# Two value tiles of cross-attention issued between the first attends instead of ahead of them

## The chip, the cores and the metric

The kernel runs on one core of a Trainium2 chip. The metric is the device time of one execution in microseconds (us). The engines named below are TensorE (PE in the rows, with its weight loads listed apart as PEld), VectorE (DVE), ScalarE (ACT), GpSimd (POOL), and SyncE (SP), which issues the DMAs. Every engine runs its own instructions in the order in which the program lists them, and the engines are held together by semaphores.

## The reference, cut to what matters

A decoder block of three parts, each followed by a layer normalisation, on `x` of 8 x 128 tokens with 512 channels: causal self-attention with 4-bit weights, cross-attention with 16 heads, and a gated expert layer. The change lies in the second part:

```python
def proj(x, W, bias):
    y = x @ W.T + bias
    return y.reshape(b, s, head_num, hd).transpose(0, 2, 1, 3).reshape(b * head_num, s, hd)
Q = proj(q, Wq, bq)
K = proj(k, Wk, bk)
V = proj(v, Wv, bv)
scores = jnp.einsum('bqd,bkd->bqk', Q, K) / jnp.sqrt(jnp.asarray(hd, jnp.float32))
attn = jax.nn.softmax(scores, axis=0)
res = jnp.einsum('bqk,bkd->bqd', attn, V)
out = res.reshape(b, head_num, s, hd).transpose(0, 2, 3, 1).reshape(b, s, hd * head_num)
```

Here `b` = 8, `s` = 128, `hd` = 32. The softmax is taken over the 128 pairs of batch entry and head (axis 0), so no tile of probabilities can be weighted before the exponentials of all eight tiles have been summed. Afterwards `x = _layernorm(x + out)`, and the third part follows:

```python
x = _layernorm(x + _L0_ffn_ref(x, ...), axis=-1)
```

## The kernel before, in words

The tokens are cut into NB = 8 tiles of 128 tokens, one for each batch entry. Self-attention takes the first three quarters of the span. In cross-attention the keys and queries are projected, the scores of the eight tiles are made (`scores2`), and VectorE takes the maxima, the shifts and the sums of the exponentials. Its chain ends in the reciprocal (L1382) and one product (L1383). Each engine's order is written out by hand; there is no planner around the change.

The parts that the steps of the prediction touch:

- **values(b)** (L1743, its matmuls at L1753) on TensorE makes the value tile b: 128 tokens by 512 channels, four fp32 matmuls, which the trace lists as eight records of 128x512. Tiles 0 to 2 take their bias from a matmul with ones (L1749). Tiles 3 to 7 add to a PSUM bank that ScalarE has filled with the bias (`seed_bias`, L1000). The bank is `proj2_bank(16 + b)`, one of banks 0 to 2 in turn. Before the change all eight are issued in a row after the last scores.
- **copy_v2(b)** (L1006, its instruction at L1010) on ScalarE copies the bank into `v2` and raises `proj2_copied`.
- **weigh(b)** (L1385, L1386) on VectorE multiplies the 128x2048 exponentials of tile b by the reciprocal sums and raises `weights2_ready`.
- **attend(b)** (L1847, L1855) on TensorE waits for `weights2_ready`, for `proj2_copied`, and for the copy of attended tile b - 2. It makes the attended tile in bank 6 or bank 4, as 32 records of 128x128.
- **copy_att(b)** (L1092, L1095) on ScalarE copies the attended tile to SBUF.
- **turn_att(b)** (L1859, L1864) on TensorE waits for that copy and for the adding of attended tile b - 1, and transposes the tile into bank 7, as four records.
- **add_attended(b)** (L1389, L1392) on VectorE waits for the transposes (`att_turned`) and adds the tile to `y`.
- **layernorm_stats** (L1274, L1278), **inverse_deviation** on GpSimd (L749, L752) and **layernorm_apply** (L1286) normalise two tiles at a time.
- **turn_x(1, b)** (L1713) transposes the normalised tile, `copy_x_t` (L981) copies it, and **gate_and_lora** (L1871) and **main** (L1880) are the first products of the expert layer.
- On SyncE the loads of the expert layer's weights (L603 to L605) wait until all 24 projection units, the eight value tiles being the last of them, are done (`proj2_done`, L602). TensorE waits for these three loads before `gate_and_lora(0)`.

VectorE's order in this stretch fixes what a late attended tile delays:

```python
weigh(0)
weigh(1)
for b in range(2, NB):
    weigh(b)
    add_attended(b - 2)
    if b % 2 == 1:
        layernorm_stats(1, b - 3, 2, attended2)
    elif b > 2:
        layernorm_apply(1, b - 4, 2)
```

So `add_attended(0)` stands behind `weigh(2)` and ahead of `weigh(3)`, and `add_attended(1)` stands behind `weigh(3)`, ahead of the first statistics and of `weigh(4)`.

Of the kernel before, what the change touches and what calls it, by code (L numbers as in the profile page):

```python
# [17 lines left out]
NB = 8  # L18
# [44 lines left out]
def wait(eng, sem, value):  # L63

    if isinstance(value, int) and value <= 0:
        return
    eng.wait_ge(sem, value)


def build(nc, t, out):  # L70
    with ExitStack() as ctx:
# [383 lines left out]
        def att_bank(b):  # L455

            return banks[6 if b % 2 == 0 else 4]
# [15 lines left out]
        def proj2_bank(i):  # L473

            if i < KC:
                return banks[7]
            if i < 2 * KC:
                return banks[(3, 4, 0, 1)[i - KC]]
            return banks[i % 3]
# [290 lines left out]
        def _(act):  # L770
# [225 lines left out]
            def exps2(b):  # L996
                act.wait_ge(shifted2, b + 1)
                nc.scalar.activation(xs[:, SLOT[b], :], xs[:, SLOT[b], :], ACT.Exp, scale=XSCALE).then_inc(exp2_done, 1)

            def seed_bias(b):  # L1000

                i = 4 * KC + b
                wait(act, proj2_copied, i - 2)
                nc.scalar.activation(proj2_bank(i), bias_v, ACT.Copy).then_inc(bias_seeded, 1)

            def copy_v2(b):  # L1006

                i = 4 * KC + b
                act.wait_ge(proj2_done, UNIT_ORDER.index(i) + 1)
                nc.scalar.activation(v2[:, b, :], proj2_bank(i), ACT.Copy).then_inc(proj2_copied, 1)  # L1010
# [73 lines left out]
            copy_v2(2)  # L1084
            seed_bias(5)
            exps2(7)
            for b in range(3, NB):
                copy_v2(b)
                if b + 3 < NB:
                    seed_bias(b + 3)  # L1090

            def copy_att(b):  # L1092
                act.wait_ge(pv2_done, b + 1)
                wait(act, att_turned, b - 1)
                nc.scalar.activation(att_t[:, b % 2, :], att_bank(b), ACT.Copy).then_inc(att_copied, 1)  # L1095

            for b in range(5):
                copy_att(b)
            copy_x_t(1, 0, x3_t)
            copy_x_t(1, 1, x3_t)  # L1100
# [415 lines left out]
        def _(pe):  # L1516
# [226 lines left out]
            def values(b):  # L1743

                i = 4 * KC + b
                first = b < 3
                if first:
                    wait(pe, proj2_copied, i - 2)
                    nc.tensor.matmul(proj2_bank(i), ones[0:1, :], bias_v[0:1, :], start=True, stop=False)  # L1749
                else:  # L1750
                    wait(pe, bias_seeded, b - 2)
                for g in range(KC):
                    mm = nc.tensor.matmul(proj2_bank(i), ctx_t[:, g, b * P:(b + 1) * P], wv2[:, g, :],  # L1753
                                          start=False, stop=not first or g == KC - 1, skip_group_check=not first)
                mm.then_inc(proj2_done, 1)
# [85 lines left out]
            for b in range(BPH):  # L1841
                scores2(BPH + b)
            pe.wait_ge(scores2_copied, NB - 1)
            for b in range(NB):
                values(b)

            def attend(b):  # L1847

                pe.wait_ge(weights2_ready, b + 1)
                pe.wait_ge(proj2_copied, 4 * KC + b + 1)  # L1850
                wait(pe, att_copied, b - 1)
                for n in range(KC):
                    for i in range(4):
                        h = 4 * n + i
                        mm = nc.tensor.matmul(att_bank(b)[32 * i:32 * i + 32, n * P:(n + 1) * P], v2[:, b, h * XD:(h + 1) * XD],  # L1855
                                              xs[:, SLOT[b], (KC * i + n) * P:(KC * i + n + 1) * P], start=True, stop=True)
                mm.then_inc(pv2_done, 1)

            def turn_att(b):  # L1859

                pe.wait_ge(att_copied, b + 1)
                wait(pe, attended2, b)
                for n in range(KC):
                    mm = nc.tensor.transpose(banks[7][:, n * P:(n + 1) * P], att_t[:, b % 2, n * P:(n + 1) * P], ident)  # L1864
                mm.then_inc(att_turned, 1)
# [23 lines left out]
                                 start=False, stop=True).then_inc(main_done, 1)  # L1889

            attend(0)
            attend(1)
            turn_att(0)
            attend(2)
            turn_att(1)
            attend(3)
# [134 lines left out]
```

## Time and profile before

| what | value |
|---|---|
| median of 3 runs | 679.2 us (676.06 to 680.47) |
| profiled execution, its own time | 676.55 us |
| its span in the trace | 674.8 us |
| TensorE busy | 639.5 us (95%) |
| VectorE busy | 556.5 us (82%) |
| ScalarE busy | 465.8 us (69%) |
| GpSimd busy | 420.9 us (62%) |
| mean granted TensorE clock | 0.992 of full speed |

All times inside the kernel are us from the start of the span. The span leaves out 1.75 us of the execution's own time. Busy shares are means over a span whose parts have different limits, so the stretch around the change is read by itself, in the rows further down.

### The profile page before, as it was taken

The numbers are of one execution on the slowest core, as the hardware profiler recorded it, in microseconds if no ns is written. First come the engines' busy times: TensorE is split into PE (matmuls) and PEld (weight loads), VectorE is DVE, ScalarE is ACT, GpSimd is POOL, SyncE is SP. The second block draws the span as 40 slices with busy tenths as digits, with TensorE's granted clock in tenths as the row PEclk, the third lists the DMA queues.
The fourth block names the chain that finished last, engine by engine and source line by source line (L and its number), as shares of the span: only waits on it lengthen the run. The fifth ranks groups of instructions, "written<-read, shape, count | busy, mean of one in ns | idle before, by whom it ended". The sixth has DMA issues, their size and how long they took to land.

```text
span 674.8 us, 11004 instructions
## 1 busy us (share of the span) xinstructions
PE 639.5 (95%) x3294; PEld 444.9 (66%) x3294; DVE 556.5 (82%) x880; ACT 465.8 (69%) x1271; POOL 420.9 (62%) x372
## 2 busy tenths in 40 slices
PE   8989999999999999999999999998998999978996
PEld 4566787877878777787777877765565444447552
DVE  5878999998999999999899989974462968998357
ACT  6697887979779797797977979776644545622100
POOL 2478899899899989989989998881230000012003
PEclk9999999999999999999999999999999998999998
DMA  7864523533351351253234124240010000020003
GB/s 232 261 166 114 154 69 96 151 109 94 110 141 46 88 165 33 59 153 90 60 111 132 43 61 114 89 127 0 1 63 0 1 1 1 0 98 2 0 1 124
DMA packets 30187, 56.72 MB, mean 84 GB/s; under 512 B 4784, under 2 KB 5040, under 8 KB 29616
## 3 DMA queue, kind: packets, MB, share of 16 engines
q1 hardware_dynamic: 30128, 56.02, 29.4%
q8 instruction: 27, 0.44, 0.3%
q14 instruction: 32, 0.26, 0.1%
HBM read 32.93 MB, written 2.10 MB: 52 GB/s over the span
## 4 chain that ended last, share of the span: by engine, by line
PE 76%; DVE 9%; ACT 4%; issue 3%; POOL 3%; DMA 2%; SPq 1%; POOLq 0%; DVEq 0%; ACTq 0%
PE ps L1527 23%; PE ps L1589 18%; PE ps L1570 8%; PE ps L1542 8%; PE ps L1597 6%; PE ps L1552 4%; PE ps L1880 3%; DMA arena<-in_qkv 2%; DVE arena L1386 2%; ACT arena L993 1%; PE ps L1770 1%; DVE arena L1359 1%; DVE late L1354 1%; DVE late L1367 1%; PE ps L1871 1%
## 5 line engine op out<-in xcount | busy, mean ns | idle before, releaser
L1140 DVE SCALAR_TENSOR_TENSOR arena<-ps,arena 128x512 f32<-128x512 f32 x288 | 212.5, 745 | 15.7 <-PE ps L1527 3.8
L1527 PE MATMUL ps<-x_hi,w_sb 128*128 128x512 f32 x384 | 170.9, 445 | 5.1 <-ACT arena L790 2.2
L1527 PE MATMUL ps<-x_lo,w_sb 128*128 128x512 f32 x384 | 150.8, 393 | 0.0
L1168 DVE SCALAR_TENSOR_TENSOR y<-ps,arena,y 128x512 f32<-128x512 f32 x192 | 138.2, 744 | 12.6 <-PE ps L1589 8.5
L799 ACT ACTIVATE arena<-ps,small 128x128 f32<-128x128 f32 x256 | 90.7, 378 | 31.3 <-DVE small L1146 26.8
L624 POOL TENSOR_TENSOR arena<-arena,consts 128x512 f32<-128x512 f32 x75 | 96.9, 1291 | 22.7 <-DVE arena L1140 22.7
L1589 PE MATMUL ps<-heads_hi,wo_sb 128*128 128x512 f32 x256 | 108.7, 425 | 0.1
L630 POOL TENSOR_TENSOR arena<-arena,consts 128x512 f32<-128x512 f32 x75 | 96.8, 1290 | 12.6 <-DMA arena<-arena 10.4
L749 POOL TENSOR_SCALAR var_eps<-mean_var 128x2 f32<-128x2 f32 (+1 forms) x13 | 7.3, 561 | 154.4 <-DVE mean_var L1278 154.4
L1589 PE MATMUL ps<-heads_lo,wo_sb 128*128 128x512 f32 x256 | 101.0, 395 | 0.0
L640 POOL TENSOR_TENSOR arena<-arena 128x512 f32<-128x512 f32 x75 | 96.6, 1287 | 5.6
L648 POOL TENSOR_TENSOR y<-arena,y 128x512 f32<-128x512 f32 x64 | 82.6, 1290 | 26.6 <-ACT arena L840 24.5
L1527 PEld LDWEIGHTS ps<-x_hi,w_sb 128*128 128x128 f32 x384 | 72.2, 188 | 39.0 <-DVE arena L1140 8.7
L790 ACT ACTIVATE arena<-ps,arena 128x512 f32<-128x512 f32 x96 | 66.6, 694 | 34.1 <-PE ps L1527 33.5
L1527 PEld LDWEIGHTS ps<-x_lo,w_sb 128*128 128x128 f32 x384 | 72.5, 189 | 16.5 <-issue 5.5
L816 ACT ACTIVATE arena<-arena,small 128x128 f32<-128x128 f32 x256 | 82.6, 419 | 0.2 <-DVE small L1152 0.2
L1570 PE MATMUL ps<-arena 128*128 128x512 f32 x128 | 66.2, 599 | 4.3 <-ACT arena L823 2.2
L1542 PEld LDWEIGHTS ps<-arena 128*128 128x128 f32 x512 | 66.2, 193 | 5.7 <-issue 1.9
L1542 PE MATMUL ps<-arena 128*128 128x128 f32 x512 | 68.0, 276 | 0.5 <-POOL arena L640 0.5
L1159 DVE TENSOR_TENSOR heads_lo<-ps,heads_hi 128x512 fp32r<-128x512 f32 x64 | 44.1, 689 | 24.4 <-ACT heads_hi L832 23.9
L1589 PEld LDWEIGHTS ps<-heads_hi,wo_sb 128*128 128x128 f32 x256 | 48.5, 189 | 16.7 <-DVE heads_lo L1159 5.6
L799 ACT ACTIVATION_READ_ACCUMULATOR arena<-ps,small 128x1 f32 x256 | 55.8, 218 | 0.0
(146 smaller groups left out, 967.6 us busy)
## 6 DMA issues: line engine op xcount, KB each, us to landing
arena<-arena SPq DMA_DIRECT2D x160, 128.0 KB, 2.3
arena<-in_qkv SPq DMA_DIRECT2D x48, 256.0 KB, 3.9
arena<-in_o SPq DMA_DIRECT2D x32, 256.0 KB, 3.7
arena<-in_x_t SPq DMA_DIRECT2D x8, 256.0 KB, 3.7
y<-in_x SPq DMA_DIRECT2D x4, 512.0 KB, 4.4
arena<-in_ctx_t SPq DMA_DIRECT2D x8, 256.0 KB, 3.1
out<-y SPq DMA_DIRECT2D x8, 256.0 KB, 2.1
arena<-in_wk SPq DMA_DIRECT2D x1, 1024.0 KB, 5.2
```

Source lines behind the costliest of these rows:

```text
L624: nc.gpsimd.tensor_tensor(by_tile(raw_cos[:, i % 2, :]), by_tile(raw[:, c % RING, :]), every_tile(cos_of(c)), ALU.mult).then_inc(cos_done, 1)
L630: nc.gpsimd.tensor_tensor(by_tile(turned[:, i % 2, :]), by_tile(turned[:, i % 2, :]), every_tile(sin_of(c)), ALU.mult).then_inc(sin_done, 1)
L640: nc.gpsimd.tensor_tensor(dst, raw_cos[:, i % 2, :], turned[:, i % 2, :], ALU.add).then_inc(rotated, 1)
L648: nc.gpsimd.tensor_tensor(dst, by_tile(out_part[:, k % 2, :]), dst, ALU.add).then_inc(part_added, 1)
L799: last = nc.scalar.activation(probs[:, s, h, :], score_ps[s][:, h * P:(h + 1) * P], ACT.Exp, bias=neg_max[:, s, h:h + 1], accum_out=row_su ...
L816: last = nc.scalar.activation(probs[:, s, h, :], probs[:, s, h, :], ACT.Copy, scale=row_inv[:, s, h:h + 1])
L1140: nc.vector.scalar_tensor_tensor(acc, group_bank(p, KC * c + g), scale_of(p // 2, c, g), acc, ALU.mult, ALU.add).then_inc(dve_scaled, 1)
L1168: nc.vector.scalar_tensor_tensor(dst, by_tile(out_bank(p, u)), out_scale_of(p // 2, u), dst, ALU.mult, ALU.add).then_inc(out_added, 1)
L1527: mm = nc.tensor.matmul(group_bank(p, u), w_sb[:, c, g, :], part[:, g, half * HALF:(half + 1) * HALF], start=(k == 0), stop=(k == 1))
L1542: mm = nc.tensor.matmul(score_ps[s][:, h * P:(h + 1) * P], q_t[:, h, b * P:(b + 1) * P], k_t[:, b * P:(b + 1) * P], start=False, stop=(n > ...
L1570: nc.tensor.matmul(pv_ps[:, :], v_sb[:, b, :], probs_t[:, s, :, :].rearrange("p h q -> p (h q)"), start=True, stop=True).then_inc(pv_done, 1)
L1589: mm = nc.tensor.matmul(out_bank(p, u), wo_sb[:, h, nt * P:(nt + 1) * P], part[:, half, h, :], start=(k == 0), stop=(k == 1))
```

## The change

On TensorE, `values(6)` moves from ahead of `attend(0)` to behind it, and `values(7)` from ahead of `attend(0)` to behind `turn_att(0)`. On ScalarE, `copy_v2(6)` moves behind `copy_att(0)` and `copy_v2(7)` behind `copy_att(1)`. `seed_bias(6)` and `seed_bias(7)` stay where they were. No instruction is added or removed, and VectorE's, GpSimd's and SyncE's programs are unchanged.

```diff
@@ ScalarE
-            for b in range(3, NB):
+            for b in range(3, 6):
                 copy_v2(b)
                 if b + 3 < NB:
                     seed_bias(b + 3)
@@
-            for b in range(5):
+            copy_att(0)
+            copy_v2(6)
+            copy_att(1)
+            copy_v2(7)
+            for b in range(2, 5):
                 copy_att(b)
@@ TensorE
-            for b in range(NB):
+            for b in range(6):
                 values(b)
@@
             attend(0)
+            values(6)
             attend(1)
             turn_att(0)
+            values(7)
             attend(2)
             turn_att(1)
             attend(3)
```

## Rows read from the trace of the kernel before

**Rows 1.** The page: busy us, share of the span, instructions; then the ending chain's shares.

```profile
PE 639.5 (95%) x3294; PEld 444.9 (66%) x3294; DVE 556.5 (82%) x880; ACT 465.8 (69%) x1271; POOL 420.9 (62%) x372
...
PE 76%; DVE 9%; ACT 4%; issue 3%; POOL 3%; DMA 2%; SPq 1%; POOLq 0%; DVEq 0%; ACTq 0%
```

**Rows 2.** The chain that ended last, 586 to 616: start, duration, what.

```profile
589.71 6.69 DVE arena L1386 x3
596.41 0.60 DVE y L1392
597.01 2.20 DVE arena L1386
599.21 0.60 DVE y L1392
...
601.30 2.15 POOL var_eps L749
...
609.56 2.15 POOL var_eps L749
...
612.51 0.56 DVE y L1286
...
613.11 0.67 PE ps L1713 x4
```

**Rows 3.** Timeline of TensorE, 572 to 606: start, duration, instruction, idle before.

```profile
572.71 20.87 PE L1753 MATMUL ps<-arena 128*128 128x512 f32 x48
593.51 1.95 PE L1855 MATMUL ps<-arena 128*32 128x128 f32 x64
595.39 0.66 PE L1864 MATMUL ps<-consts,late 128*128 128x128 f32 x4
596.46 1.08 PE L1855 MATMUL ps<-arena 128*32 128x128 f32 x32 [0.41 <-DVE arena L1386]
597.47 0.66 PE L1864 MATMUL ps<-consts,late 128*128 128x128 f32 x4
599.26 1.08 PE L1855 MATMUL ps<-arena 128*32 128x128 f32 x32 [1.13 <-DVE arena L1386]
...
603.45 1.08 PE L1855 MATMUL ps<-arena 128*32 128x128 f32 x32 [2.52 <-DVE arena L1386]
```

**Rows 4.** Busy time by stretch: length, engines, granted clock, DMA share, GB/s.

```profile
469.50:472.90 3.40, 3.40 (x15) 3.01 (x13) 0.75 (x1) 0.83 (x2) 0.06 (x1) 0.50 0.00 0
561.65:565.07 3.42, 3.42 (x5) 1.51 (x5) 3.39 (x2) 0.69 (x1) 0.00 (x0) 0.50 0.00 0
...
599.20:602.60 3.40, 1.67 (x36) 1.24 (x36) 3.40 (x7) 0.60 (x1) 1.30 (x1) 1.00 0.04 13
...
668.70:670.90 2.20, 0.00 (x0) 0.00 (x0) 1.99 (x5) 0.00 (x0) 0.83 (x2) 1.00 0.64 238
670.90:674.80 3.90, 0.00 (x0) 0.00 (x0) 0.65 (x2) 0.00 (x0) 0.70 (x2) 0.50 0.36 134
```

**Rows 5.** Timeline of TensorE: a gap in self-attention, then value tiles 0 and 1.

```profile
468.42 1.12 PE L1570 MATMUL ps<-arena 128*128 128x512 f32 x2 [2.15 <-ACT arena L823]
...
561.68 5.37 PE L1753 MATMUL ps<-arena 128*128 128x512 f32 x8
...
568.03 3.70 PE L1753 MATMUL ps<-arena 128*128 128x512 f32 x8
```

**Rows 6.** The expert weights' last load and its landing, and the first gate product.

```profile
L605 SPq DMA_DIRECT2D arena<-in_w_b x1: 432/432/432, 594.5 to 594.5; - x1
...
DMA to landing us min/median/max: 5.4/5.4/5.4
...
606.76 1.25 PE L1871 MATMUL ps<-arena 128*128 128x160 f32 x8
```

**Rows 7.** Busy time by stretch, columns as in rows 4: the attends, the expert layer.

```profile
593.50:613.10 19.60, 13.55 (x269) 10.88 (x268) 19.07 (x23) 5.63 (x10) 5.67 (x4) 1.00 0.23 85
613.10:654.70 41.60, 38.97 (x213) 25.39 (x213) 22.46 (x75) 6.49 (x13) 3.41 (x5) 1.00 0.00 1
```

## The prediction

> **What bounds the kernel now.** I read the page first. TensorE is busy for 95% of the span and carries 76% of the chain that ended last [rows 1], which would suggest that anything that frees TensorE pays. But that is a mean over the whole span, and the change sits in one stretch of 20 us, so the second view is the chain in order of time around it. There the end is not set by TensorE: from 589.71 to 613.07 the chain lies on VectorE, with two visits to GpSimd for the deviations (the one at 601.30 and a second like it at 609.56), and TensorE takes it over only at 613.11 [rows 2]. What the reader is to see in that view is the order weigh(0), weigh(1), weigh(2) (6.69 us for the three), add_attended(0), weigh(3), add_attended(1), with no gap between them. The third view, the sums by stretch, says the same: from 593.5 to 613.1 VectorE is busy for 19.07 of 19.60 us and TensorE for 13.55; from 613.1 to 654.7 it is TensorE with 38.97 of 41.60 [rows 7]. The fourth view is TensorE's own timeline, for how near it runs to the chain. Value tiles 2 to 7 end at 593.51, where attend(0) starts at once, and turn_att(0) runs from 595.39 to 596.05 [rows 3]. VectorE is free for add_attended(0) at 596.41. So the transposed tile 0 is ready only 0.36 us before it is wanted, and tile 1 (597.47 to 598.13) 1.08 us before 599.21 [rows 2, 3]. Whatever is put ahead of these two transposes on TensorE beyond that slack is paid by VectorE.
>
> **What the change takes away.** Six value tiles, 48 records, take 593.51 - 572.71 = 20.80 us, or 3.47 us each [rows 3]. With tiles 6 and 7 moved, the values end at 593.51 - 6.93 = 586.58. Can this pull anything forward? attend(0) needs weigh(0), which starts at 589.71 and takes 6.69 / 3 = 2.23 us, so it ends at 591.94 and attend(0) can start at about 592.00, 1.5 us earlier than before. Nothing on the chain follows from that, since add_attended(0) stands behind weigh(2), which ends at 596.40 whatever TensorE does. VectorE's softmax chain does not read the value tiles, so weigh(0) doesn't come earlier. The part that is removed is worth 0, and it opens a gap on TensorE from 586.58 to 592.00, 5.4 us.
>
> **What it adds, at full clock.** The pair of attends takes 1.95 us for 64 records, so one holds TensorE for 0.98 us [rows 3]. attend(0) runs from 592.00 and values(6) from 592.98 to 596.45, which passes the end of weigh(2). Then attend(1) holds TensorE to 597.43, and turn_att(0), which now stands behind both, takes 0.66 us and ends at 598.09. add_attended(0) starts then instead of at 596.41: VectorE stands still for 1.7 us. Next, the issue of turn_att(0) frees TensorE after 0.6 us, at 598.0; values(7) runs to 601.5, attend(2) to 602.5, and turn_att(1) ends at 603.1. On VectorE add_attended(0) and weigh(3) take 0.60 + 2.20 us [rows 2] and end at 600.9, so add_attended(1) waits another 2.2 us, and starts at 603.15 instead of 599.21. The delay is now 3.9 us. It isn't 2 x 3.47, because the 1.5 us by which attend(0) starts earlier and the slack of 1.1 us before add_attended(1) come off, and some of the seams differ by tenths; I take **+4.0**.
>
> Behind add_attended(1) nothing makes it good. VectorE goes on with the statistics of tiles 0 and 1, weigh(4) and the rest in the same order, each of which was back to back before [rows 2, 7]; GpSimd starts from those statistics; attend(4) waits for weigh(4), as before (its idle of 2.52 us was ended by VectorE) [rows 3]; and turn_x(1, 2) at 613.11, from which TensorE sets the end, is released by the normalising at 612.51 [rows 2]. From there to the end TensorE is almost full, so the delay goes through one to one.
>
> **ScalarE and SyncE.** Each copy_v2 now stands in front of one copy_att. copy_v2(6) waits for values(6), and attend(1) is behind values(6) on TensorE anyway, so copy_att(1) isn't later for it; the same holds for copy_v2(7) and copy_att(2). Cost 0, covered by TensorE's own order. If that cover failed, 0.6 us a copy would be the price. The loads of the expert weights are issued when the last value tile is done: that moves from 593.5 to 601.5, by 8 us. Before, the last of the three was issued at 594.5 and landed 5.4 us later, at 599.9, and the gate product that needs it began at 606.76 [rows 6]. After, it lands at 607.9 at full clock and the gate product is due at 606.76 + 4.0 = 610.8. The slack shrinks from 6.9 to 2.9 us but is not gone. Cost 0; with a landing twice as long, 5.4 us more, it would be 2.5.
>
> **The clock.** The 5.4 us gap is new, and it has a price of its own. In self-attention a gap of 2.15 us before 468.42 was followed by the lower level (0.50, 1.2 GHz) from 469.50 to 472.90, and after the last matmul the clock was at 0.50 from 670.90, 2.2 us into the idle time. Against that, the idle of 2.52 us before 603.45 cost nothing: the clock stayed at 1.00 (2.4 GHz) [rows 3, 4, 5]. So gaps of this size go either way; one of 5.4 us, twice as long as any of the three, I expect to bring the clock down. Its price comes from value tile 0, which ran in such a stretch: 5.37 us against 3.70 us for tile 1 at full clock, **+1.67 us** [rows 4, 5]. Both low stretches with dense work in them lasted 3.4 us. If the whole of such a stretch falls on attend(0) and values(6), all of 1.67 us goes in front of turn_att(0) and so into the chain. Bounds: 0 from below (no fall, as before 603.45), and twice 1.67 = 3.3 from above (still low after the first stretch, as at the end of the trace, where it is at 0.50 for 3.90 us with no matmul). I take 1.67, the row with dense work.
>
> How this weighs for attend(0), no row shows, as no attend ran at the lower clock. The Trainium skill, page "TensorE: Matmul & The Clock Gate", section "Wait — 56ns, not 53.3ns?", gives a floor of about 25 ns from one start to the next for small matmuls; attend's records come every 0.98 us / 32 = 31 ns, near it. By that rule attend(0) would not slow down, and of the 3.4 us low only the 2.4 us in values(6) would cost, half of them: an estimate of 1.2 us in place of 1.67. The sum would be 0.5 us smaller; the sum below doesn't use it.
>
> **Sum.** 0 (removed) + 4.0 (two transposes late) + 1.7 (clock) = +5.7 us. Against the profiled execution's own time, 676.55 + 5.7 = 682.3. That execution is on the low side of the runs shown (676.06, 679.2, 680.47). With it there are four, whose middle is (676.55 + 679.2) / 2 = 677.9; +5.7 gives **683.5 us**, 0.8% more. A change of 1%, 6.8 us, is about what a measurement of this kernel can tell from none.
>
> **The rivals.**
>
> A, *the clock stays up*: only the +4.0. For it: the 2.52 us gap without a fall. Against it: the new gap is over twice that. Time 677.9 + 4.0 = 681.9. Chance 0.13.
>
> B, *a second fall of the clock*. The gap before attend(4), 2.5 us long, stays, and now comes after other work, so that it may be judged as the 2.15 us gap was. Or the first low stretch runs longer. Another 1.67 on attend(4) and what follows, or in the dense part after 613: 677.9 + 4.0 + 3.3 = 685.2, slower by 1.1%. For it: the gaps of 1.13 and 2.52 us in this part [rows 3]. Against it: neither brought a fall before. Chance 0.18.
>
> C, *the other side: TensorE's idle time swallows the two tiles*. TensorE has 19.60 - 13.55 = 6.05 us idle between 593.5 and 613.1 [rows 7], nearly the 6.93 us of two tiles, and attend(0) starts 1.5 us earlier. The place is the wait of add_attended(0), and the point from which it decides is 596.41: if turn_att(0) were through by then and turn_att(1) by 599.21, VectorE would lose nothing, and if the early attends then let TensorE run ahead, up to 1.5 us would be won, 677.9 - 1.5 = 676.4. Against it: turn_att(0) stands behind values(6) in program order, values(6) alone ends at 596.45, and the idle time lies mostly after 600. Chance 0.06, gain and no change together.
>
> D, *the expert weights come late*: the gate product waits for the loads. Its point is a landing after 610.8; the slack is 2.9 us, and the delay on both sides grows alike with the clock. With a landing twice as long +2.5 us: 686.0. Chance 0.03.
>
> **How the numbers follow.** My forecast has 0.60, A 0.13, B 0.18, C 0.06, D 0.03. The forecast at +5.7, with the clock's price anywhere from 0.8 to 2.5, lies just below the 6.8 us of 1%, so about a quarter of it (0.14) comes out slower by over 1%; with 0.13 of B's 0.18 and D's 0.03 that makes 0.30. Faster by over 1% would need more than any step can give: 0.02. The rest, 0.68, is within 1%. The range goes from A less the spread of the runs (681.9 - 2.9 = 679.0) to the far end of the clock with that spread, 677.9 + 4.0 + 3.3 + 2.3 = 687.5. It leaves out most of C.
>
> **What would show it right or wrong.** In the profile after: attend(0) starts near 592.0 with an idle time of about 5 us before it, released by VectorE's weigh(0); the granted clock is at 0.50 for a stretch around 590 to 596; add_attended(0) and add_attended(1) show idle times before them, released by TensorE's L1864, of about 1.7 and 2.2 us at full clock, together 3.5 to 5.7 with the clock's part; turn_x(1, 2) comes 4 to 7.5 us after 613.11; what lies behind it keeps its length. The prediction is wrong if VectorE shows no such waits, if the gate product waits for a DMA, or if the part behind turn_x(1, 2) gets shorter by what was lost.

## The result, and the profile after

The changed kernel takes 685.45 us (median of 4 runs, 684.27 to 685.6) against 678.36 us for the kernel before (median of 4, 676.06 to 680.47): 7.1 us more. The ratio is 1.0102, with a 95% interval of 1.0077 to 1.0127. The profiled execution took 685.44 us, its span is 683.7 us. The forecast was 683.5 us in a range of 679.0 to 687.5.

The page of the kernel after, busy time by engine and the shares of the ending chain, beside [rows 1]:

```profile
PE 643.3 (94%) x3294; PEld 447.3 (65%) x3294; DVE 557.2 (82%) x880; ACT 466.1 (68%) x1271; POOL 421.4 (62%) x372
...
PE 77%; DVE 8%; ACT 4%; issue 3%; POOL 3%; DMA 2%; SPq 1%; POOLq 0%; DVEq 0%; ACTq 0%
```

The same instructions run; TensorE is busy 3.8 us longer for the same work, which already hints at a lower clock. The chain that ended last shows where the time is (line numbers behind the edit are 4 higher than before):

```profile
591.50 2.30 DVE arena L1390
593.80 0.04 issue
593.84 1.94 PE ps L1859 x32
595.78 5.53 PE ps L1757 x8
601.31 1.01 PE ps L1859 x32
602.32 0.59 PE ps L1868 x4
602.91 3.44 PE ps L1757 x8
606.34 1.01 PE ps L1859 x32
607.35 0.60 PE ps L1868 x4
607.95 0.02 issue
607.98 0.69 DVE y L1396
...
621.98 0.67 PE ps L1717 x4
```

Before, this stretch was VectorE alone: three weighs, add_attended(0), weigh(3), add_attended(1) [rows 2]. Now it goes from weigh(0) through attend(0), values(6), attend(1), turn_att(0), values(7), attend(2) and turn_att(1), all on TensorE, and returns to VectorE at add_attended(1). A chain that moves to another engine for 14 us is the sign of a wait that was not there before. The timeline of VectorE shows the two waits by name; the bracket is the idle time and what ended it:

```profile
591.50 6.70 DVE L1390 TENSOR_TENSOR arena<-arena,small 128x2048 f32<-128x2048 f32 x3
602.94 0.69 DVE L1396 TENSOR_TENSOR y<-ps,y 128x512 f32<-128x512 f32 x1 [4.75 <-PE ps L1868]
603.55 2.28 DVE L1390 TENSOR_TENSOR arena<-arena,small 128x2048 f32<-128x2048 f32 x1
607.98 0.69 DVE L1396 TENSOR_TENSOR y<-ps,y 128x512 f32<-128x512 f32 x1 [2.14 <-PE ps L1868]
```

4.75 + 2.14 = 6.9 us of VectorE's time, ended by the transposes of turn_att(0) and turn_att(1). TensorE's timeline shows the gap that the moved tiles left, 7.01 us, and values(6) behind it:

```profile
572.83 14.00 PE L1757 MATMUL ps<-arena 128*128 128x512 f32 x32
593.84 1.94 PE L1859 MATMUL ps<-arena 128*32 128x128 f32 x32 [7.01 <-DVE arena L1390]
595.71 5.60 PE L1757 MATMUL ps<-arena 128*128 128x512 f32 x8
601.24 1.08 PE L1859 MATMUL ps<-arena 128*32 128x128 f32 x32
602.25 0.66 PE L1868 MATMUL ps<-consts,late 128*128 128x128 f32 x4
602.74 3.60 PE L1757 MATMUL ps<-arena 128*128 128x512 f32 x8
```

attend(0) takes 1.94 us where attend(1) takes 1.08, and values(6) 5.60 us where values(7) takes 3.60. The sums by stretch say why; columns as in [rows 4], the granted clock third from the end:

```profile
586.80:589.30 2.50, 0.03 (x1) 0.00 (x0) 2.40 (x4) 0.60 (x1) 0.00 (x0) 1.00 0.00 0
589.30:593.80 4.50, 0.00 (x0) 0.00 (x0) 4.33 (x7) 0.00 (x0) 0.00 (x0) 0.50 0.00 0
593.80:599.50 5.70, 5.66 (x37) 3.12 (x38) 4.39 (x2) 0.60 (x1) 0.00 (x0) 0.50 0.00 0
599.60:608.00 8.40, 8.40 (x88) 4.40 (x91) 2.92 (x3) 2.37 (x4) 0.00 (x0) 1.00 0.06 12
613.30:616.60 3.30, 3.00 (x17) 2.59 (x14) 3.30 (x4) 1.20 (x2) 0.00 (x0) 0.50 0.00 2
```

The clock fell to 0.50 (1.2 GHz) some 2.5 us into the gap, and stayed there for the first 5.7 us of the work behind it.

**A measure that scatters less than the span.** I cut each span in three: up to the start of weigh(0), from there to the start of turn_x(1, 2), where TensorE takes over for good, and the rest. Before, that is 589.71, 23.40 and 61.7 us; after, 591.50, 30.48 and 61.7 us. The middle part grew by 7.08 us. The span grew by 8.9 us because this execution also came to weigh(0) 1.79 us later; whether that belongs to the change is one of the things tested below.

### The profile page after: what moved, and what is told of

It is laid out like the page before. It is cut to its first block, busy times and chain, and to the rows that moved or that the text cites. A ratio compares the mean times of both kernels' runs of the same rounds, so it can differ in the third digit from the quotient of the medians.

```text
span 683.7 us, 11004 instructions
## 1 busy us (share of the span) xinstructions
PE 643.3 (94%) x3294; PEld 447.3 (65%) x3294; DVE 557.2 (82%) x880; ACT 466.1 (68%) x1271; POOL 421.4 (62%) x372
## 4 chain that ended last, share of the span: by engine, by line
PE 77%; DVE 8%; ACT 4%; issue 3%; POOL 3%; DMA 2%; SPq 1%; POOLq 0%; DVEq 0%; ACTq 0%
PE ps L1531 23%; PE ps L1593 17%; PE ps L1574 8%; PE ps L1546 8%; PE ps L1601 6%; PE ps L1556 4%; PE ps L1884 3%; DMA arena<-in_qkv 2%; ACT arena L993 1%; PE ps L1757 1%; DVE arena L1363 1%; PE ps L1774 1%; DVE late L1358 1%; DVE late L1371 1%; PE ps L1875 1%
## 5 line engine op out<-in xcount | busy, mean ns | idle before, releaser
L630 POOL TENSOR_TENSOR arena<-arena,consts 128x512 f32<-128x512 f32 x75 | 96.9, 1292 | 14.5 <-DMA arena<-arena 13.1
```

What stands on the lines that cost most here:

```text
L630: nc.gpsimd.tensor_tensor(by_tile(turned[:, i % 2, :]), by_tile(turned[:, i % 2, :]), every_tile(sin_of(c)), ALU.mult).then_inc(sin_done, 1)
```

## The experiments

Theory: two costs, nothing else. The order costs about 4 us, because turn_att(0) and turn_att(1) now stand behind value tiles and VectorE waits for them; the clock costs about 3 us, because the gap brings it down. Rivals: the order alone costs 7 us and the clock nothing; TensorE is the bound here and any work moved costs its length; a part of the 7 us arises ahead of weigh(0). All kernels ran beside the kernel before. "Stretch" is weigh(0) to turn_x(1, 2); each row is one profiled execution, all columns in us.

| kernel | weigh(0) starts | to add_attended(0) | on to add_attended(1) | stretch | rest |
|---|---|---|---|---|---|
| before | 589.71 | 6.62 | 2.80 | 23.40 | 61.7 |
| before, again | 592.61 | 6.62 | 2.79 | 23.41 | 61.7 |
| after | 591.50 | 11.44 | 5.04 | 30.48 | 61.7 |
| after, again | 592.15 | 11.68 | 5.04 | 30.71 | 61.6 |
| after, gap filled | 593.40 | 8.70 | 5.03 | 27.73 | 61.7 |
| tile 7 alone, behind turn_att(0) | 593.18 | 6.61 | 4.68 | 25.29 | 61.6 |
| tile 7 alone, behind turn_att(1) | 590.75 | 7.57 | 2.80 | 24.36 | 61.7 |
| tile 6 alone | 591.45 | 11.59 | 2.81 | 28.39 | 61.7 |
| tile 6 alone, gap filled | 593.88 | 8.70 | 2.80 | 25.49 | 61.6 |
| tiles 6 and 7 left out | 591.82 | 7.17 | 2.80 | 23.96 | 61.6 |
| GpSimd weighs tiles 3 and 5 | 593.65 | 15.26 | 3.15 | 32.94 | 61.3 |
| the same, tile 7 behind turn_att(1) | 592.36 | 15.26 | 3.15 | 34.96 | 61.4 |

**1. The gap filled.** The kernel after, with matmuls that keep TensorE at work:

```diff
+            for k in range(6):
+                nc.tensor.matmul(banks[3], ctx_t[:, k % KC, 0:P], wv2[:, k % KC, :], start=True, stop=True)
             attend(0)
             values(6)
```

> The kernel after, with six fp32 matmuls of 128x512 into the free bank 3 (0.86 us each, 5.1 us) between value tile 5 and attend(0), where TensorE stood idle for 7.0 us. Their results are not used. Theory (two causes, order and clock): the granted clock stays at 1.00 up to attend(0) and behind it, attend(0) takes 1.0 us and values(6) 3.4 us instead of 1.94 and 5.53; the stretch from the start of weigh(0) to the start of turn_x(1, 2), 23.40 us before and 30.48 us after, is 27.5 us; the time is 4.1 us over the kernel before. Rival (order alone; the low clock costs nothing on the path): 30.5 us and +7.1 us.

Measured: 684.26 us against 679.0, ratio 1.0071 (1.0051 to 1.0091). The stretch is 27.73 us, 2.75 us shorter than after and 4.33 us longer than before. TensorE's timeline in this kernel, from the filler on:

```profile
588.57 5.31 PE L1896 MATMUL ps<-arena 128*128 128x512 f32 x12
595.75 1.08 PE L1859 MATMUL ps<-arena 128*32 128x128 f32 x32 [1.87 <-DVE arena L1390]
596.76 3.70 PE L1757 MATMUL ps<-arena 128*128 128x512 f32 x8
```

and its sums by stretch, with the clock at 1.00 in both:

```profile
593.90:595.70 1.80, 0.00 (x0) 0.00 (x0) 1.80 (x2) 0.00 (x0) 0.00 (x0) 1.00 0.00 0
595.70:602.10 6.40, 6.35 (x77) 3.75 (x78) 4.40 (x2) 1.75 (x3) 0.00 (x0) 1.00 0.00 0
```

attend(0) is back at 1.08 us and values(6) at 3.70 us, with more work on TensorE than before. This run separates the two costs: the order 4.3 us, the clock 2.75 us. A kernel that does more is faster by 2.75 us in the stretch. On the medians the two kernels lie about 2 us apart (+7.1 and +5.3), with intervals that overlap, so the size of each cost rests on the stretches. The interval by itself, +3.5 to +6.2 us, holds the 4.1 us of the theory and not the 7.1 us of the rival.

**2. Tile 7 alone, behind turn_att(0).**

```diff
-            for b in range(NB):
+            for b in range(7):
                 values(b)
@@
             attend(1)
             turn_att(0)
+            values(7)
             attend(2)
```

> Only value tile 7 is moved, behind turn_att(0) as in the change; tile 6 is made ahead of attend(0) as before. Theory: turn_att(0) is on time, turn_att(1) is about 1.75 us late for add_attended(1); the gap before attend(0) is 3.5 us or less, so a fall of the clock adds between 0 and 1.7 us: +1.7 to +3.4 us, the stretch from weigh(0) to turn_x(1, 2) 25.1 to 26.8 us. Rival (all of the change's cost comes from values(6) ahead of attend(1)): +0.

Measured: 681.89 us against 679.0, ratio 1.005 (1.0033 to 1.0068); stretch +1.89 us. In the profiled execution the gap before attend(0) was only 1.89 us, since value tile 0 had run at the lower clock (5.40 us in place of 3.70) and ended the value tiles later; behind the gap the clock stayed up. add_attended(0) is on time, add_attended(1) is 1.88 us late. So values(6) is not the whole cost. The interval, +2.2 to +4.6 us, lies above this one stretch.

**3. Tile 7 alone, behind turn_att(1).** The edit is the same but for the place (copy_v2(7) moves with it, behind copy_att(2)):

```diff
             turn_att(0)
             attend(2)
             turn_att(1)
+            values(7)
             attend(3)
```

> Only value tile 7 is moved, but behind turn_att(1) instead of turn_att(0); the gap ahead of attend(0) is the same as in the run with tile 7 behind turn_att(0). Theory (what counts is what stands ahead of a transpose that VectorE waits for): turn_att(1) has 1.1 us of slack, turn_att(2) ends 0.1 us before it is wanted, so 0 at full clock and up to +1.2 with a low stretch of the clock. Rival (a tile moved out of the front costs its 3.5 us wherever it stands, as TensorE is the bound): +1.7 to +3.5 us.

Measured: 678.12 us against 679.0, ratio 0.9992 (0.998 to 1.0003): no difference. The same tile leaves the same place and costs nothing in the runs, one transpose further down: what counts is what stands ahead of a transpose that VectorE waits for. The gap was not the same as in the last run, as its text had assumed: here value tile 0 ran at full clock, and the gap was 3.58 us. It was followed by a low clock, which made turn_att(0) late by 0.87 us; that is the +0.96 us of this stretch. TensorE's timeline holds one more thing:

```profile
593.09 1.93 PE L1858 MATMUL ps<-arena 128*32 128x128 f32 x32 [3.58 <-DVE arena L1389]
...
609.92 1.35 PE L1874 MATMUL ps<-arena 128*128 128x160 f32 x8 [1.00 <-DMA arena<-in_w_b]
```

The first gate product (L1874) waits 1.00 us for the last of the expert weights, whose load was issued at 604.5 and not at 594.5. That is the wait of my rival D. It costs nothing here: VectorE shows no wait for TensorE in this part, and the rest behind turn_x(1, 2) keeps its 61.7 us.

**4. Tiles 6 and 7 left out.** The kernel before without the eight fp32 matmuls of value tiles 6 and 7; their banks are copied with the bias alone. The two waits for all 24 units, on SyncE and on ScalarE, are lowered to 22, and only the first is shown. The kernel leaves out a part of the result.

```diff
-            for b in range(NB):
+            for b in range(6):
                 values(b)
@@
-            sp.wait_ge(proj2_done, UNITS)
+            sp.wait_ge(proj2_done, UNITS - 2)
```

> The kernel before, with value tiles 6 and 7 not computed at all (their banks, holding the bias alone, are copied), so that attend(0) follows value tile 5: 6.9 us less work on TensorE and the same gap before attend(0) as in the kernel after. Theory (VectorE is the bound from weigh(0) to turn_x(1, 2)): no gain, -0.5 to +1.0 us, where a cost comes from attend(0) and attend(1) at the lower clock. Rival (TensorE, 95% busy, is the bound here too): -6.9 us.

Measured: 678.91 us against 679.0, ratio 0.9995 (0.9978 to 1.0012). 6.9 us of TensorE's work less buys nothing (the interval is -1.5 to +0.8 us): VectorE is the bound in this stretch, and TensorE's 95% on the page says nothing about it. The stretch is +0.56 us, from a low clock behind a gap of 5.32 us, which made turn_att(0) late by 0.47 us:

```profile
594.17 1.93 PE L1857 MATMUL ps<-arena 128*32 128x128 f32 x32 [5.32 <-DVE arena L1388]
596.37 1.93 PE L1857 MATMUL ps<-arena 128*32 128x128 f32 x32 [0.27 <-DVE arena L1388]
```

**5. Tile 6 alone, between attend(0) and attend(1).** Tile 7 is made ahead of attend(0); the order of the units and of the copies follows.

```diff
-UNIT_ORDER = list(range(UNITS))
+UNIT_ORDER = list(range(UNITS - 2)) + [23, 22]
@@
-            for b in range(NB):
+            for b in [0, 1, 2, 3, 4, 5, 7]:
                 values(b)
@@
             attend(0)
+            values(6)
             attend(1)
```

> Only value tile 6 is moved, between attend(0) and attend(1); tile 7 is made ahead of attend(0), in front of it. Theory: turn_att(0) is 1.7 us late for add_attended(0); the 1.1 us of slack before add_attended(1) and the rest of the order hide nothing of it, since VectorE runs back to back behind it; the gap before attend(0) is 1.9 to 3.5 us, so up to 1.7 us more for the clock: +1.7 to +3.4 us, the stretch from weigh(0) to turn_x(1, 2) 25.1 to 26.8 us. Together with the +1.9 us of tile 7 alone that gives less than the 4.3 us of both at full clock. Rival (one tile is swallowed by the gap it leaves, 1.5 us earlier start of attend(0)): +0.

Measured: 682.86 us against 678.39, ratio 1.0066 (1.0045 to 1.0087); stretch +4.99 us. That is above what the theory allowed. The clock was low behind a gap of 3.58 us, and attend(0) and values(6) took 1.93 and 5.75 us, so most of the surplus looked like the clock; I had allowed 1.7 us for it. The next run tests that.

**6. Tile 6 alone with the gap filled.** The same with three such filler matmuls ahead of attend(0).

> Value tile 6 alone moved between attend(0) and attend(1), with three fp32 matmuls of 128x512 into the free bank 3 (2.6 us) in the gap before attend(0); their results are not used. Theory: the gap shrinks from 3.6 to about 1 us, the clock stays at 1.00, attend(0) takes 1.0 us and values(6) 3.4 us in place of 1.93 and 5.75: the stretch from weigh(0) to turn_x(1, 2) is 25.2 us in place of 28.39, the time +1.8 us over before. Rival (the order alone makes the 5.0 us of this tile): 28.4 us and +4.5 us.

Measured: 681.45 us against 678.38, ratio 1.0042 (1.0025 to 1.0059); stretch 25.49 us, +2.09. The clock stayed up behind a gap of 1.01 us, and attend(0) and values(6) took 1.08 and 3.70 us. So for tile 6 the order costs 2.1 us and the clock 28.39 - 25.49 = 2.9 us. The medians lie closer together, +4.5 and +3.1 us; the second interval, +1.7 to +4.0 us, leaves out the 4.5 us of the rival. At full clock tile 6 costs 2.1, tile 7 1.9, and both together 4.3 us.

**7. The kernels before and after once more.**

> The kernel before, unchanged, for a second profile of it. Theory (the start of weigh(0) scatters from run to run, whatever the order behind it, and the first profile of before was an early one): weigh(0) starts between 591 and 593.5 us, later than 589.71, and the stretch from there to turn_x(1, 2) is 23.4 us again, with 61.7 us behind it. Rival (the change also delays what stands ahead of weigh(0)): weigh(0) starts near 589.7 again.

> The kernel after, unchanged, on the same chip as the three others. Theory: +7 us as in the first measurement, the stretch from weigh(0) to turn_x(1, 2) about 30.5 us with a low clock behind the gap; the clock's part can differ from run to run between 1.2 and 3.1 us, so 28.8 to 30.7. Rival (the first measurement's 3 us for the clock was chance): under 29 us and +5 us.

Measured: before, 679.47 us, one run; weigh(0) starts at 592.61, the stretch is 23.41 us. After, 686.56 us against 678.39, ratio 1.0105 (1.008 to 1.0131); weigh(0) at 592.15, stretch 30.71 us, attend(0) at 1.94 and values(6) at 5.83 us. The kernel before came to weigh(0) later in its second profile, at 592.61, than the kernel after in either of its own. So the 1.79 us ahead of weigh(0) is no cost of the change, and the first profile of before was the earliest of all (the table has 589.71 to 593.88). That is why I had to set its time beside the median. The stretch and the rest repeat within 0.3 us in the two profiles that each of these kernels has.

What the stretches leave open is 1 to 2 us in the time of a whole execution. The second comparison of after gives +8.2 us on the medians and +7.1 by its ratio, and its six runs split into four of 686.3 to 687.8 us and two of 682.9 and 683.2. With the gap filled the medians are 1 us above the stretch, for both tiles (+5.3 and +4.33) and for tile 6 (+3.1 and +2.09). For tile 7 alone the whole interval misses the stretch, above it behind turn_att(0) (+2.2 to +4.6, stretch +1.89) and below it behind turn_att(1) (-1.4 to +0.2, stretch +0.96). Other executions may have had another clock, or another start of weigh(0); no run here separates the two.

**8. VectorE relieved.** Since VectorE is the bound, I gave two of its eight weighs to GpSimd, which stands idle there, on top of the kernel before (attend(3) and attend(5) then wait for GpSimd, which is not shown):

```diff
+            pool.wait_ge(soft_step, 33)
+            for b in (3, 5):
+                weighed = xs[:, SLOT[b], :].rearrange("p (g q) -> p g q", q=P)
+                nc.gpsimd.tensor_tensor(weighed, weighed, x_r[b // BPH].unsqueeze(1).broadcast_to([P, 16, P]),
+                                        ALU.mult).then_inc(pool_weighed, 1)
@@
-                weigh(b)
+                if b not in (3, 5):
+                    weigh(b)
```

> The kernel before, with weigh(3) and weigh(5) taken from VectorE and done by GpSimd, which stood idle up to 601: both 128x2048, of four 128x512 at 1.29 us each, so some 5.2 us a tile, done 10.3 us after the sums are ready. Theory (VectorE sets the pace from weigh(0) to turn_x(1, 2)): add_attended(1) comes about 1 us earlier, held then by turn_att(1), and weigh(5) leaves 2.2 us less behind it: the stretch falls from 23.4 to 20.3 us, -2 to -3.2 us. Rival (TensorE sets it): 0. Second rival (the two engines slow each other on SBUF): weigh on VectorE takes clearly longer than 2.2 us and the gain goes.

> Both together: weigh(3) and weigh(5) on GpSimd, and value tile 7 behind turn_att(1). Theory: once VectorE is relieved, turn_att(2) behind value tile 7 is what is late, so the tile costs 0 to 1 us at full clock and up to 1.7 us more with the clock low; -0.5 to -3 us against the kernel before, no better than the run with GpSimd alone. Rival (a relieved VectorE makes TensorE the bound and the late tile pays for its 1.5 us earlier start): better than GpSimd alone by 1 us or more.

Measured: 689.19 us against 678.39, ratio 1.0142 (1.0123 to 1.0161), and with the late tile 7 690.35 us, ratio 1.0168 (1.0153 to 1.0184). The gain that both texts expected did not come; the second rival of the first text holds. The late tile made nothing better, so the rival of the second text falls. Its stretch is 2.0 us longer, and here the chain that ended last runs through the late loads: values(7), then the last load of expert weights with 5.47 us to its landing, then the first gate product, which waited 1.49 us for it. The timeline of GpSimd and VectorE in the first of the two:

```profile
593.65 15.34 DVE L1392 TENSOR_TENSOR arena<-arena,small 128x2048 f32<-128x2048 f32 x3
593.69 13.15 POOL L765 TENSOR_TENSOR arena<-arena,small 128x2048 f32<-128x2048 f32 x2 [79.86 <-DVE small L1389]
```

The same three weighs on VectorE take 6.70 us in the kernel after and 15.34 us here. This says nothing against VectorE being the bound. The three weighs became 8.64 us longer, the two that left VectorE took some 4.4 us off, and two waits for transposes behind attends at the lower clock, of 2.47 and 2.05 us, came on: 8.8 of the 9.5 us by which the stretch grew. It only shows that GpSimd cannot take this work from VectorE in this form. No version was faster than the kernel before by more than the noise.

## Why the prediction was right, point by point

- **VectorE bounds the stretch, TensorE only from turn_x(1, 2).** Right. 6.9 us of TensorE's work left out gained nothing, and the rest behind turn_x(1, 2) is 61.6 to 61.7 us in every order of the attends, so the delay goes through one to one.
- **What is removed is worth 0.** Right, by the same run.
- **The waits.** They came where the prediction put them, ended by the transposes. Their sum, 4.75 + 2.14 = 6.9 us, is above the 3.5 to 5.7 that it gave as a sign, and the surplus is the clock's, below.
- **The order, +4.0.** It measured 4.3 us at full clock. The waits of VectorE are 2.00 us for add_attended(0), where I had 1.7, and 2.14 for add_attended(1), where I had 2.2; the rest is in the seams. One reason that I gave is a chance of one profile: attend(0) could start 1.5 us earlier only because the value tiles had ended late in it. In the second profile of before, attend(0) already started 2.35 us behind the start of weigh(0), as it does after the change (2.34). The slack ahead of the two transposes was the same there, 0.4 and 1.0 us, and it is the slack that sets the cost.
- **The clock, +1.67.** The fall came as forecast, but its size was too small: 2.75 us in the first profile, by the run with the gap filled, and about 2.9 us for tile 6 alone. Two things went wrong in "I take 1.67, the row with dense work". The gap is 7.0 us and not 5.4: in the first profile of before, value tile 0 ran at the lower clock, which put the end of all value tiles 1.67 us late; in the kernel after it did not. And I took over the length of a low stretch, 3.4 us, with all of it on dense work. Here it lasted from 589.3 to about 599.6, of which the last 5.7 us fell on work; half of that is 2.85 us. In the second profile of after, the fall came some 3 us into the gap, 6.1 us of work were at the lower clock, and attend(0) and values(6) took 0.2 us more. The price lies inside my bounds of 0 and 3.3.
- **attend(0) at the lower clock.** The Trainium skill, page "TensorE: Matmul & The Clock Gate", section "Wait — 56ns, not 53.3ns?", gives the floor of about 25 ns between starts; that attends at 31 ns a record would therefore keep their pace at the lower clock was my reading of it. attend(0) went from 1.08 to 1.94 us, so the row decides against that reading, and the sum was right not to use it.
- **The sum.** 4.3 + 2.75 = 7.05 us, measured 7.09 on the medians; that they agree to the tenth is luck, as the medians of the second comparison differ by 8.2. My +5.7 was 1.4 short: 1.1 of it the clock, 0.3 the order. The rest of the distance to 685.45 is my starting point, 677.9, where the kernel before measured 678.36. The longer low stretch is rival B in its second form, "the first low stretch runs longer", whose 685.2 us is nearer to the 685.45 measured than the 683.5 of the likeliest case.
- **Rival B, a second fall.** It came too, from 613.3 to 616.6, and cost nothing: VectorE shows no wait for TensorE there. I had priced it as if every low stretch were on the chain.
- **The chances.** I gave 0.68 to a change within 1% and 0.30 to one slower by more. The ratio is 1.0102 (1.0077 to 1.0127), on the edge and by its middle on the less likely side. That 1% is about what a measurement of this kernel can tell from none was too cautious: with 4 to 12 runs the intervals here reach 0.12 to 0.26% to either side.
- **Rival A**, the clock stays up, is what the filler makes: 27.73 us. **Rival C** fell, since the transposes were not through in time. **Rival D** did not occur in the kernel after: the loads landed at 607.2 + 6.8 = 614.0 us and the gate product came at 616.50. The wait did show with tile 7 behind turn_att(1): off the chain on the kernel before, and on the chain together with GpSimd's weighs.
- **ScalarE, cost 0.** Right: copy_v2(6) and copy_v2(7) end before the attended tile they stand ahead of is there.

## What to carry to other kernels

Before work is moved "into idle time" of a busy engine, look for the transposes or copies behind the place that another, fully loaded engine waits for, and compare their slack (here 0.36 and 1.08 us) with the length of what is put ahead of them; one place further down the same tile cost nothing. Price the hole it leaves as well: here each of the six gaps of 3.58 us or more before attend(0) brought TensorE's clock down, and the work behind it paid. And where the whole span scatters by 4 us, measure the change in the stretch between two fixed instructions, which repeated here within 0.3 us, and keep the medians beside it: a stretch is one execution, with the clock that this one happened to have.

## What the runs showed of the hardware that I had not expected

**The clock behind gaps.** In the profiles, gaps on TensorE of 1.01, 1.87 and 1.89 us before attend(0) left it at 1.00. Gaps of 3.58 (three times), 5.32 and 7.01 us (twice) each brought it to 0.50. The low stretches lasted 10.2 us behind the longest gaps and 6.8 us behind the shorter ones, but for one gap of 3.58 us that was soon followed by a second of 4.58 us, again 10.2 us. Gaps of 2.5 to 2.8 us before attend(4) went both ways, for the same program: no fall in the first profile of before, a fall in the second. A long gap isn't even needed. In 3 of the 12 profiles (before, tile 7 alone behind turn_att(0), tiles 6 and 7 left out) the clock was at 0.50 for the 3.4 us of value tile 0, behind idle times of 1.1 us at most between the last scores; in the other 9, with the same instructions up to there, it was not. This decides whether the value tiles ahead of attend(0) end 1.7 us later, and with it how long the gap before attend(0) is. Work of all shapes slowed: attend from 1.08 to 1.94 us, values(6) from 3.70 to 5.60 us with some two thirds of it at the lower clock.

**VectorE and GpSimd on SBUF.** A weigh reads two operands from SBUF. With GpSimd doing the same beside it, the two engines took turns. The starts of the attends show when each weigh of VectorE ended in that run:

```profile
596.00 1.08 PE L1864 MATMUL ps<-arena 128*32 128x128 f32 x32
...
602.52 1.94 PE L1864 MATMUL ps<-arena 128*32 128x128 f32 x32 [5.44 <-DVE arena L1392]
...
609.04 1.93 PE L1864 MATMUL ps<-arena 128*32 128x128 f32 x32 [3.56 <-DVE arena L1392]
```

weigh(0) ended just before 596.00, after its usual 2.3 us, although GpSimd had begun 0.04 us behind it; weigh(1) and weigh(2) came 6.5 us apart each. The two tiles of GpSimd took 13.15 / 2 = 6.6 us each. If a weigh of VectorE needs 2.23 us alone, 6.5 - 2.23 = 4.3 us are left for one of GpSimd. This 4.3 is an estimate, as no run has GpSimd weighing alone. By strict turns each tile of GpSimd then waits for one weigh of VectorE, 2 x (2.23 + 4.3) = 13.1 us, where 13.15 were measured. Sharing by halves would have slowed weigh(0) too. The second run with GpSimd repeats both totals, 15.34 and 13.15 us. The Trainium skill, page "SBUF — State Buffer", section "SBUF: two separate sides", states that a VectorE instruction with two SBUF inputs, against a GpSimd instruction that reads SBUF, takes a shared pair of ports exclusively, and that whichever starts first has it for the whole instruction; the trace agrees. I had expected a partial slowdown at most.
